# One matmul and three small DMAs place each row of negated maxima in the query operand

## What is computed

```
scores = jnp.einsum('bhqd,bhkd->bhqk', q, k) * scale
attn = jax.nn.softmax(scores, axis=-1)
out = jnp.einsum('bhqk,bkhd->bqhd', attn, v)
```

## Time and profile before

| what | us |
|---|---|
| median of three runs | 3212.43 |
| the profiled execution | 3212.74 |
| its span, first to last instruction | 3210.7 |
| TensorE busy (matmuls) | 3098.2 |
| VectorE busy | 2834.2 |
| ScalarE busy | 2504.5 |
| GpSimd busy | 262.0 |

### The profile page before, as it was taken

The page is one execution under the profiler, slowest core; times in us unless marked ns, Lnnn a source line. Parts: engine busy times, 40 slices in busy tenths (PEclk is TensorE's granted clock), DMA queues, the critical chain, the costliest instruction groups (busy, mean ns, idle before and its releaser), DMA issues.

```text
span 3210.7 us, 70961 instructions
## 1 busy us (share of the span) xinstructions
PE 3098.2 (96%) x26983; PEld 1357.5 (42%) x26983; DVE 2834.2 (88%) x3108; ACT 2504.5 (78%) x4551; POOL 262.0 (8%) x810
## 2 busy tenths in 40 slices
PE   8999999999999999999999999999999999998883
PEld 4544444444444444344444334444444434465652
DVE  5599999999999999999999999999999999356666
ACT  5288888888888888888888888888888888733333
POOL 2400000000000000000000000000000000101103
PEclk9799999999999999999999999999999999989996
DMA  7320202010101010101010101011010110000001
GB/s 255 59 41 1 41 1 41 1 41 2 41 1 37 5 34 8 34 8 31 11 27 14 24 18 24 18 21 21 18 24 14 27 30 1 1 0 0 0 0 52
DMA packets 27354, 82.72 MB, mean 26 GB/s; under 512 B 4641, under 2 KB 15633, under 8 KB 24018
## 3 DMA queue, kind: packets, MB, share of 16 engines
q1 hardware_dynamic: 26818, 77.84, 10.5%
q0 software_dynamic: 272, 1.05, 0.1%
HBM read 57.90 MB, written 20.97 MB: 25 GB/s over the span
## 4 chain that ended last, share of the span: by engine, by line
PE 94%; DVE 2%; issue 1%; ACT 1%; POOL 0%; DVEq 0%; POOLq 0%; ACTq 0%
PE ps L1022 41%; PE ps L1031 36%; PE ps L1235 4%; PE ps L998 3%; PE ps L957 2%; PE ps L1184 2%; PE ps L1041 1%; PE ps L1224 1%; PE ps L1159 1%; PE ps L971 1%; PE ps L1049 1%; PE ps L949 1%; DVE partial L750 1%; ACT q_raw L619 0%; PE ps L1201 0%
## 5 line engine op out<-in xcount | busy, mean ns | idle before, releaser
L750 DVE TENSOR_REDUCE partial<-ps 128x1 f32<-128x1024 f32 x2048 | 2482.4, 1223 | 123.7 <-PE ps L998 101.7
L577 ACT ACTIVATE work<-ps 128x512 f32<-128x512 f32 x4096 | 2207.6, 596 | 344.7 <-PE ps L1022 136.6
L998 PE MATMUL ps<-k_stack,q_stack 48*128 48x512 f32 x4096 | 1532.6, 453 | 4.9 <-DVE partial L750 4.2
L1022 PE MATMUL ps<-q_stack,k_stack 64*128 64x512 f32 x4096 | 1510.2, 448 | 0.5 <-ACT work L577 0.5
L1031 PE MATMUL ps<-work,v_head 128*32 128x256 f32 x16384 | 1296.1, 391 | 0.0
L1022 PEld LDWEIGHTS ps<-q_stack,k_stack 64*128 64x128 f32 x4096 | 632.2, 184 | 807.6 <-ACT work L577 676.5
L998 PEld LDWEIGHTS ps<-k_stack,q_stack 48*128 48x128 f32 x4096 | 634.3, 187 | 46.1 <-DVE partial L750 40.8
L1031 PEld LDWEIGHTS ps<-work,v_head 128*32 128x32 f32 x16384 | 329.1, 108 | 697.2 <-ACT work L577 581.5
L423 POOL CAST nm_parts<-negmax 128x4 bf16<-128x4 f32 x128 | 25.0, 195 | 2272.6 <-DVE negmax L757 2272.6
L1235 PE MATMUL ps<-k_raw,q_raw 128*128 128x256 f32 x512 | 127.6, 406 | 17.8 <-ACT q_raw L619 17.8
L619 ACT ACTIVATE q_raw<-ps 128x1024 f32<-128x1024 f32 x32 | 32.8, 1025 | 132.6 <-PE ps L1224 132.6
(11 more groups left out here) (128 smaller groups left out, 1074.4 us busy)
## 6 DMA issues: line engine op xcount, KB each, us to landing
k_stack<-qk_parts SPq DMA_DIRECT2D x96, 256.0 KB, 4.1
q_stack<-qk_parts SPq DMA_DIRECT2D x96, 256.0 KB, 4.1
qk_parts<-qk_part SPq DMA_DIRECT2D x32, 512.0 KB, 2.8
x_sb<-L_attn_x SPq DMA_DIRECT2D x8, 512.0 KB, 10.8
out<-work SPq DMA_DIRECT2D x8, 512.0 KB, 2.9
k_raw<-L_ffn_aux_values SPq DMA_DIRECT2D x1, 1024.0 KB
work<-L_attn_w_qkv POOLq DMA_DIRECT2D x1, 768.0 KB, 7.3
q_raw<-L_ffn_aux_keys SPq DMA_DIRECT2D x1, 512.0 KB
```

The source lines that it names most:

```text
L577: act.activation(probs[:, g % DEPTH, a, :], ps[:, bank, :], ACT.Exp, scale=SCALE).then_inc(exp_done, 1)
L750: dve.tensor_reduce(partial[:, k // 4, k % 4:k % 4 + 1], ps[:, 2 * slot:2 * slot + 2, :], AX.XY, ALU.max).then_inc(max_used, 1)
L998: last = pe.matmul(ps[:, 2 * slot + e, :], q_stack[HALF:HALF + ROWS, b1, c * CH + (k // 4) * P:c * CH + (k // 4 + 1) * P], k_stack[HALF:HA ...
L1022: pe.matmul(ps[:, bank, :], k_stack[0:HALF, b, P * g:P * (g + 1)], q_stack[0:HALF, b, at:at + CH], start=True, stop=True).then_inc(s_ready, 1)
```

## The change

Seven edits belong together.

- `LEAD` goes from 8 to 10, so the maxima are two pieces further ahead, `ROW_STEPS` from (15, 29) to (13, 27), and `COMB_AFTER` follows to 17.
- `nm_parts` is laid out part by part, so that all 12 columns (3 parts of 4 tiles) are one operand.
- `max_row` issues one matmul with 12 columns of weights and 128 columns of the identity. It gives 12 x 128 numbers in one bank.
- ScalarE copies 12 x 128 into `row_stage`, one of two places by the row's parity (`stage_max_row`), after the DMAs that read this place before are done.
- SyncE places them in `q_stack` (`place_rows`): for each of three parts a DMA of 4 partitions x 128 into one partition of 512. The semaphores are `row_in[0]` and `row_in[1]`.
- The first score of each half of a pass waits for `row_in`, where it waited for `mrow_done`. The ring's wait for a row's bank stays on `mrow_done`.
- SyncE's list is rewritten pass by pass: the loads of the next head keep their counts of `pv_done`, row 0 of the next pass stands ahead of the fifth load of a pass (s = 4), row 1 behind all of them, and the weights' loads at the start of the last head.

```diff
--- before.py
+++ after.py
@@ -56,14 +56,14 @@
     AHEAD = 2
     PAIRS = NC // 2
     ITS = H * PAIRS
-    LEAD = 8
+    LEAD = 10
     DEPTH = 4
     LAG = 2
     QH = CH // 2
     SRING = 3
     S_BANK = [4, 5, 6]
     O_BANK = 7
-    ROW_STEPS = (15, 29)
+    ROW_STEPS = (13, 27)
     COMB_STEP = 7
     COMB_AFTER = LEAD + COMB_STEP
     ring = []
@@ -119,7 +119,8 @@
         partial = sb("partial", [P, TPC, 4])
         negmax = sb("negmax", [P, TPC])
         nm_rest = sb("nm_rest", [P, 2, TPC])
-        nm_parts = sb("nm_parts", [P, TPC, MROWS], BF16)
+        nm_parts = sb("nm_parts", [P, MROWS, TPC], BF16)
+        row_stage = sb("row_stage", [MROWS * TPC, 2, P])
         rinv = sb("rinv", [P, 2, 4])
         lead = sb("lead", [P, 1])
 
@@ -222,6 +223,7 @@
         comb_used = sem("comb_used")
         mrow_ready = sem("mrow_ready")
         mrow_done = sem("mrow_done")
+        row_in = [sem(f"row_in{m}") for m in range(2)]
 
 
         dve_passed = sem("dve_passed")
@@ -304,41 +306,64 @@
                         sp.dma_start(stack[SLOT_ROW[n]:SLOT_ROW[n] + D, 1, 0:T].bitcast(F32),
                                      parts_dram[qk, part, 0:D, :]).then_inc(done, 16)
 
-            def load_stack(h, b, after):
-                for n, (row, pq, pk) in enumerate(zip(SLOT_ROW, SLOT_Q, SLOT_K)):
-                    for m, (stack, qk, part) in enumerate(((k_stack, 1, pk), (q_stack, 0, pq))):
-                        sp.wait_ge(pv_done, after + (2 * n + m) * LOAD_EVERY)
-                        sp.dma_start(stack[row:row + D, b, 0:T].bitcast(F32), parts_dram[qk, part, h * D:(h + 1) * D, :]
-                                     ).then_inc(stack_in[b], 16)
+            def load_part(h, b, k, after):
+
+                n, m = k // 2, k % 2
+                stack, qk, part = ((k_stack, 1, SLOT_K[n]), (q_stack, 0, SLOT_Q[n]))[m]
+                sp.wait_ge(pv_done, after + CREDIT[pv_done])
+                sp.dma_start(stack[SLOT_ROW[n]:SLOT_ROW[n] + D, b, 0:T].bitcast(F32),
+                             parts_dram[qk, part, h * D:(h + 1) * D, :]).then_inc(stack_in[b], 16)
+
+            def place_rows(n, b):
+
+                c, m = n % NC, n % 2
+                sp.wait_ge(mrow_done, n + 1 + CREDIT[mrow_done])
+                for r in range(MROWS):
+                    dst = q_stack[MROW + r:MROW + r + 1, b, c * CH:(c + 1) * CH].bitcast(F32)
+                    sp.dma_start(dst.rearrange("r (i t) -> r i t", i=TPC), row_stage[TPC * r:TPC * (r + 1), m, :]
+                                 ).then_inc(row_in[m], 16)
 
             for g in (0, 2, 1, 3):
                 sp.wait_ge(parts_out[g], 16 * (NC + 1))
                 if g == 2:
                     load_first((3, 4, 5), first_max_in)
                     load_first((0, 1, 2), first_score_in)
-            load_stack(1, 0, 1 + CREDIT[pv_done])
-            for h in range(2, H):
-                load_stack(h, (h + 1) % NB, (h - 1) * PAIRS * KG + CREDIT[pv_done])
-
-            sp.wait_ge(pv_done, (ITS - PAIRS) * KG + CREDIT[pv_done])
-            sp.wait_ge(w3_init, 2)
-            for dst, src in (
...
-            ):
-                sp.dma_start(dst, src, allow_slow_non_contiguous=True).then_inc(w3_in, 16)
+            def load_weights():
+
+                sp.wait_ge(pv_done, (ITS - PAIRS) * KG + CREDIT[pv_done])
+                sp.wait_ge(w3_init, 2)
+                for dst, src in (
...
+                ):
+                    sp.dma_start(dst, src, allow_slow_non_contiguous=True).then_inc(w3_in, 16)
+
+            place_rows(0, 1)
+            place_rows(1, 1)
+            for it in range(ITS - 1):
+                h, j = it // PAIRS, it % PAIRS
+                if h == H - 1 and j == 0:
+                    load_weights()
+                following = ((it + 1) // PAIRS + 1) % NB
+                for s in range(KG // LOAD_EVERY):
+                    k = j * (KG // LOAD_EVERY) + s
+                    if s == 4:
+                        place_rows(2 * it + 2, following)
+                    if h + 1 < H and k < LOADS:
+                        load_part(h + 1, h % NB, k, it * KG + max(1, s * LOAD_EVERY))
+                place_rows(2 * it + 3, following)
 
             with sp.Fori(0, NC // 2) as c2:
                 for b in range(2):
@@ -420,17 +445,17 @@
                 pool.wait_ge(negmax_ready, mi + 1 + CREDIT[negmax_ready])
                 pool.wait_ge(mrow_ready, mi + CREDIT[mrow_ready])
                 pool.sem_inc(pool_passed, 1)
-                pool.tensor_copy(nm_parts[:, :, 0], negmax[:, :]).then_inc(pool_own, 1)
+                pool.tensor_copy(nm_parts[:, 0, :], negmax[:, :]).then_inc(pool_own, 1)
                 pool.wait_ge(pool_own, mi * 4 + 1)
-                pool.tensor_tensor(nm_rest[:, 0, :], negmax[:, :], nm_parts[:, :, 0], ALU.subtract).then_inc(pool_own, 1)
+                pool.tensor_tensor(nm_rest[:, 0, :], negmax[:, :], nm_parts[:, 0, :], ALU.subtract).then_inc(pool_own, 1)
                 pool.wait_ge(pool_own, mi * 4 + 2)
                 pool.sem_inc(pool_passed, 1)
-                pool.tensor_copy(nm_parts[:, :, 1], nm_rest[:, 0, :]).then_inc(pool_own, 1)
+                pool.tensor_copy(nm_parts[:, 1, :], nm_rest[:, 0, :]).then_inc(pool_own, 1)
                 pool.wait_ge(pool_own, mi * 4 + 3)
-                pool.tensor_tensor(nm_rest[:, 1, :], nm_rest[:, 0, :], nm_parts[:, :, 1], ALU.subtract).then_inc(pool_own, 1)
+                pool.tensor_tensor(nm_rest[:, 1, :], nm_rest[:, 0, :], nm_parts[:, 1, :], ALU.subtract).then_inc(pool_own, 1)
                 pool.wait_ge(pool_own, mi * 4 + 4)
                 pool.sem_inc(pool_passed, 1)
-                pool.tensor_copy(nm_parts[:, :, 2], nm_rest[:, 1, :]).then_inc(nmparts_ready, 1)
+                pool.tensor_copy(nm_parts[:, 2, :], nm_rest[:, 1, :]).then_inc(nmparts_ready, 1)
 
             with pool.Fori(0, AHEAD) as c:
                 split_max(c)
@@ -562,12 +587,13 @@
             evacuate_v(NC - 2)
             evacuate_v(NC - 1)
 
-            def move_max_row(b, c, n, m):
+            def stage_max_row(n, m):
 
                 act.wait_ge(mrow_ready, n + 1 + CREDIT[mrow_ready])
+                if n >= 2:
+                    act.wait_ge(row_in[n % 2], (n // 2) * (16 * MROWS))
                 bank = S_BANK[(row_at[m] if n is not m else m - 2) % SRING]
-                act.activation(q_stack[MROW:MROW + MROWS, b, bass.ds(c * CH, CH)], ps[0:MROWS, bank, :],
-                               ACT.Copy).then_inc(mrow_done, 1)
+                act.activation(row_stage[:, n % 2, :], ps[0:MROWS * TPC, bank, 0:P], ACT.Copy).then_inc(mrow_done, 1)
 
             def exponential(g, a, it):
                 if a == 0:
@@ -588,7 +614,7 @@
                         exponential(g, a, it)
                     if g in ROW_STEPS and next_row:
                         m = ROW_STEPS.index(g)
-                        move_max_row(next_row[0], next_row[1] + m, it * 2 + (2 + m), m)
+                        stage_max_row(it * 2 + (2 + m), m)
                     if g in move_after:
                         move_aT(move_after[g])
                 if next_row:
@@ -600,15 +626,14 @@
                 act.activation(o_sb[:, :], ps[:, O_BANK, 0:QH], ACT.Copy).then_inc(o_evac, 1)
 
             act.wait_ge(rows_set, 2)
-            move_max_row(1, 0, 0, 0)
-            move_max_row(1, 1, 1, 1)
+            stage_max_row(0, 0)
+            stage_max_row(1, 1)
             for g in range(LAG):
                 for a in range(2):
                     exponential(g, a, 0)
 
             for it in range(ITS - 1):
-                h, j = (it + 1) // PAIRS, (it + 1) % PAIRS
-                attend(it, ((h + 1) % NB, 2 * j))
+                attend(it, True)
             attend(ITS - 1, None, {17: 0, KG - 1: 1})
 
 
@@ -1016,7 +1041,7 @@
             def score(g, a, it, b, j, rows):
 
                 if g == 0:
-                    pe.wait_ge(mrow_done, it * 2 + (a + 1 + CREDIT[mrow_done]))
+                    pe.wait_ge(row_in[a], (it + 1) * (16 * MROWS))
                 bank = bank_free(it, score_at[2 * g + a], rows)
                 at = j * (2 * CH) + a * CH
                 pe.matmul(ps[:, bank, :], k_stack[0:HALF, b, P * g:P * (g + 1)],
@@ -1045,10 +1070,8 @@
             def max_row(n, bank):
 
                 pe.wait_ge(nmparts_ready, n + 1 + CREDIT[nmparts_ready])
-                for i in range(TPC):
-                    last = pe.matmul(ps[0:MROWS, bank, P * i:P * (i + 1)], nm_parts[:, i, :], ident_bf[:, :],
-                                     start=True, stop=True)
-                last.then_inc(mrow_ready, 1)
+                pe.matmul(ps[0:MROWS * TPC, bank, 0:P], nm_parts[:, :, :].rearrange("p r i -> p (r i)"), ident_bf[:, :],
+                          start=True, stop=True).then_inc(mrow_ready, 1)
 
             def step(g, it, b, j, ahead, before):
```

(20 more changed lines are left out.)

## The result

The changed kernel takes 3265.45 us in the median of four runs (3255.18 to 3270.15), the one before 3212.66 beside it: the ratio of the means is 1.0159, with a 95% interval of 1.0135 to 1.0184. The forecast was 3255, with a range of 3228 to 3276, and slower. The profiled execution took 3270.15 us, with a span of 3268.2: 57.5 us more than the 3210.7 of before. Behind the last combine all these kernels run the same code, and their profiled executions take from 393.6 us (e3) to 406.3 us (e9) for it, at differing granted clocks of TensorE (mean 1.00 from 2861 to 2921 us in e3, 0.89 before), so where a few us count I compare the 64 passes in the profiles and not the medians.

A forecast was written before the change was run, and what follows sets the result against it. It took TensorE, with 94% of the chain of waits, as the bound. Row matmuls 0, combine lag 15.1, stands 21.8 and start 5.9 summed to +42.8 us on 3212.7: forecast 3255 us, range 3228 to 3276.

The forecast's parts named there:

- The row matmuls: At each row step, three fewer matmuls gain 0, since the second score waits for ScalarE's exponential; ends 0 and 21.4 us.
- The lag at the combine: LEAD 10 puts a small VectorE operation ahead of the combine: 0.24 us in 63 passes, 15.1 us lost.
- The placing: Row 1's DMAs queue behind a load in the first pass of 15 heads; TensorE stands, 21.8 us lost, other passes nothing.
- The term 1.45 us: TensorE's stand, with the signal, at the second score after each of 15 heads' first passes; 1.45 x 15 = 21.8 us.
- my two reasons: Third small DMA lands at 1521.15, 2.8 us after issue, or not before 1521.17, behind the load's own 4.1 us.
- rival 2: Small placing DMAs as slow as loads, 4.1 us each, with stalls in every pass: 3291 us; chance 8%.
- my row of 2.8: Profile row for a DMA out of SBUF, 2.8 us, taken as the landing time of a small placing DMA.
- the estimate worked out from it, 3243: With about 2.0 us fixed per DMA, third lands at 1520.35, stall 0.65, sum 12 us lower: 3243.
- the DMA's ends of 0 and 40 us: Range of the loss by stands: 0 if the third landed in 1.4 us, 40 if a small DMA took 4.1.
- The start: Before the first pass, two more pieces and one uncovered placing of row 1 cost 5.9 us together.
- the two pieces: At the start, LEAD 10 makes two more pieces before the first step: 2.5 us.
- the bare placing: At the start, row 1's placing is uncovered once; the score waits 3.4 us (1.3 to 4.7).

The follow-up runs named there:

- e3: Changed kernel with row 1 placed ahead of the pass's last load and LEAD back at 8: 3215.06 us, ratio 1.0002 to the kernel before.
- e9: Kernel before with only the combine moved behind step 3 (COMB_STEP 3): 3199.04 us, ratio 0.9962.
- e5: e3 with the new 12-column row matmul issued four times, same result each time: 3215.01 us, ratio 1.0000 to the kernel before.
- e6: e3 without the row matmul and the row's place in the ring of banks; maxima don't reach the scores: 3177.88 us, ratio 0.9890 to the kernel before.
- e2: Changed kernel with LEAD back at 8, nothing else changed: 3270.34 us, ratio 1.0182 to the kernel before.
- e4: Kernel before with LEAD 10 alone, rows still made by four matmuls and copied by ScalarE: 3230.61 us, ratio 1.0056.
- e7: Changed kernel with the pass's last load cut: 16 KB ahead of row 1's placing, 240 KB behind it: 3244.07 us, ratio 1.0096 to the kernel before.

## Why the prediction was right, and where its sizes were off

**The row matmuls: right.** The step that decided the sign was to ask what ends the row step, and not how much work TensorE has in it. The forecast was 2.73 us with ScalarE as the cause, the trace shows 2.74 with the exponential (L603) at the end of the wait, e5 adds the three matmuls again for nothing, and e6 takes 34 to 37 us out with the bank's place. The copy is 251 ns, shorter than the 290 of the forecast, and changes nothing.

**The lag at the combine: right, 16.0 instead of 15.1.** The forecast of 0.22 to 0.24 us holds for the passes of 41.27; in the others the small reduction started 0.12 us after the reduction before it had ended, not 0.03, and the lag was 0.32. What makes these differ is open. e2 and e4 tie the lag to LEAD from both sides.

**The placing: right in place and number, too small in size.** The 15 stands are where they were forecast, and the 48 other passes have none. The term 1.45 us was 1.85. Most of the difference is the issue: a small DMA takes SyncE 0.58 us and the third starts 1.60 us behind the load, where I had 1.28 from the issues of big loads. The rest is the 0.1 us that a pass loses beyond the stand itself. The landing of 2.8 us after the third issue was right, 2.75 in the mean of the 15, but only one of my two reasons for it holds, and that the other came to the same end was luck. Behind the load a small DMA lands late, as I had it from the load's own landing. By itself it is faster than any row that I had: at the start, where no load is ahead, the last of the three is issued at about 166.4 and the score goes on at 168.10.

```profile
165.18 1.80 SPq L323 DMA_DIRECT2D q_stack<-row_stage  x3
...
168.10 0.79 PE L1047 MATMUL ps<-q_stack,k_stack 64*128 64x512 f32 x1 [2.47 <-DMA q_stack<-row_stage]
```

So it takes 1.7 us alone and 2.5 to 3.1 behind 256 KB, and rival 2, slow small DMAs, is out. The 2.0 us fixed that the Trainium skill (DMA: Bandwidth & Descriptors, Anatomy of one DMA) gives for GpSimd's path is nearer to the 1.7 than my row of 2.8. But the estimate worked out from it, 3243, left out the load in front, which costs 1.15 us at each stand. What the Trainium skill (the same page, Queues, rings and completion order) says of descriptors consumed in ring order fits: e7 leaves order and wait as they are and takes 240 KB from the front, and 1.15 us go. In the prediction's numbers two things don't come out: the DMA's ends of 0 and 40 us give 3234 to 3274 and not 3238 to 3270, and the passes of the kernel before repeat to 0.1 us and not to 0.01 (41.0 to 41.1, two of 41.33).

**Not in the prediction: the clock.** It is 8.1 us of the profiled execution, and no term of the sum had it. Whether it is also why the four runs spread over 15 us isn't shown: one of them was profiled, and runs of the kernel before, which has no stands, spread over 17 us beside e9. A stand at the turn of a pass, with TensorE idle for 1.5 to 1.9 us, was followed by a fall to the lower level in two of 15 cases, in e2 in ten of 15, and the idle of 0.4 us in e7 in none of 15. The length of the idle doesn't tell which: in e2 falls follow 1.45 to 1.97 us of it, and none follows 1.45 to 1.72 us of it in the other five. Why the one kernel falls more often than the other, with the same stands, isn't settled by these runs.

**The start: right in sum, 5.6 against 5.9, in part by luck.** The parts can be read from the first row's copy to the second score of the first pass, which are 11.04 us before (151.69 to 162.73) and 15.94 after (152.16 to 168.10). With LEAD 10 alone (e4) they are 13.59, with the placing alone (e3) 13.39:

```profile
152.24 0.59 ACT L569 ACTIVATE q_stack<-ps 3x512 fp32r<-3x512 f32 x1 [39.87 <-PE ps L1049]
165.83 0.79 PE L1022 MATMUL ps<-q_stack,k_stack 64*128 64x512 f32 x1
...
151.81 0.27 ACT L597 ACTIVATE row_stage<-ps 12x128 f32<-12x128 f32 x1 [39.56 <-PE ps L1074]
165.20 0.79 PE L1048 MATMUL ps<-q_stack,k_stack 64*128 64x512 f32 x1 [2.47 <-DMA q_stack<-row_stage]
```

So the two pieces are 2.55 us, where I had 2.5, and the bare placing 2.35, where I had 3.4 from a landing that was too long. The other 0.7 us of the 5.6 come before and behind this stretch, and no term of mine had them. The first combine is a worse mark: TensorE is at the lower level in this stretch and rises at another point in each kernel, so e3 and e5, which differ there only by matmuls, have it at 177.34 and 179.25.

## What to carry to other kernels

Before counting a removed operation as a gain, find what starts the next one: here a buffer's turn in a ring held the place of the work, and three matmuls less, or three more, made no difference. A transfer that something waits for belongs ahead of bulk loads in its queue, since it inherits both the wait of the load in front and its bytes; and after shifting work by a lead or an offset, look which small operation has moved in front of a wait. A stand of the bounding engine can cost more than its length, if its clock falls after it.

## What the runs showed of the hardware

- Three DMAs of 2 KB from SBUF to SBUF cost SyncE 1.82 us to issue, 0.6 each, where a load of 256 KB takes 0.31 alone.
- One such DMA takes 1.7 us from issue to the waiting matmul, also behind 16 KB (e7), and 2.5 to 3.1 behind a load of 256 KB.
- After TensorE had stood idle for 1.45 to 1.97 us in a stretch that is otherwise dense, the granted clock fell to half in 12 of 30 cases (the changed kernel and e2), for a loss of 1.2 to 4.2 us each time; after 0.4 us of idle (e7) it never did.
- ScalarE's copy of 128 columns takes 251 ns, of 256 columns 390 and of 512 columns 587, all from PSUM; the 128 columns take 293 ns from SBUF (e6).
